# Four graph layers on one core: layer 1's activations from GpSimd with two column operands, orders drawn anew

## The reference

```python
h = jnp.maximum(_layernorm(x, axis=-1), 0.0)
x = x + _L0_gnn_ref(h, adj, ...)   # deg*(h Wi + b) + adj @ (h Wj)
h = jnp.maximum(_layernorm(x, axis=-1), 0.0)
x = x + _L1_gnn_ref(h, adj, ...)   # graph attention: softmax(leaky(src_i + dst_j)) @ (h W)
h = jnp.maximum(_layernorm(x, axis=-1), 0.0)
x = x + _L2_gnn_ref(h, adj, ...)   # graph attention on 128 features, beside h W itself
h = jnp.maximum(_layernorm(x, axis=-1), 0.0)
x = x + _L3_gnn_ref(h, adj, ...)   # attention with 8 heads, masked by adj
```

## Time and profile before

| what | before |
|---|---|
| median of three runs | 1237.13 us (1236.1 to 1239.11) |
| profiled execution: its own time | 1239.31 us |
| profiled execution: span from first to last instruction | 1237.2 us, granted TensorE clock 0.994 |
| busy: PE, PEld | 1193.5 us (96%), 1101.4 us (89%) |
| busy: POOL | 1137.0 us (92%) |
| busy: ACT, DVE | 1099.5 us (89%), 1092.9 us (88%) |
| DMA | 78.59 MB, 64 GB/s in the mean |

### The profile page before, as it was taken

One profiled execution on the slowest core, in us unless ns is written; L12 is line 12 of the kernel. 1 busy time (PEld: TensorE's weight loads), 2 busy tenths in 40 slices (PEclk: granted clock), 3 DMA queues, 4 the chain that ended last, 5 costly groups with the idle time before them and its releaser, 6 DMA issues. The chain is left out here.

```text
span 1237.2 us, 44146 instructions
## 1 busy us (share of the span) xinstructions
PE 1193.5 (96%) x12017; PEld 1101.4 (89%) x12017; DVE 1092.9 (88%) x5524; ACT 1099.5 (89%) x4040; POOL 1137.0 (92%) x1857
## 2 busy tenths in 40 slices
PE   6889999999999999999999999999999999999997
PEld 5678999998999898998999999899989999999986
DVE  6889999989999898998999999899989999998773
ACT  3559999999999899998999998999989999999986
POOL 5989999999999999999999999999999999998774
PEclk9999999999999999999999999999999999999999
DMA  7220342433333344343343344244344234421001
GB/s 189 64 63 13 69 74 60 68 75 53 70 74 57 67 75 56 65 77 55 66 76 55 70 74 58 67 73 60 67 71 68 64 67 71 64 46 23 19 20 35
DMA packets 97682, 78.59 MB, mean 64 GB/s; under 512 B 31648, under 2 KB 89248, under 8 KB 97440
## 3 DMA queue, kind: packets, MB, share of 16 engines
q1 hardware_dynamic: 94960, 74.07, 32.9%
q10 hardware_dynamic: 2480, 1.71, 0.5%
HBM read 58.79 MB, written 16.95 MB: 61 GB/s over the span
## 5 line engine op out<-in xcount | busy, mean ns | idle before, releaser
L1347 ACT ACTIVATE exps<-masked,nmax 128x128 f32<-128x128 f32 x1024 | 398.0, 397 | 9.9 <-issue 6.7
L497 POOL TENSOR_TENSOR probs<-exps,rsum 128x512 f32<-128x512 f32 x256 | 266.6, 1043 | 14.9 <-DVE rsum L909 14.9
L901 DVE CUSTOM_DVE_ANT_0 masked<-bank,mask 128x128 f32<-128x128 f32 x1024 | 225.3, 285 | 6.7 <-PE bank L1736 6.2
L768 DVE BATCH_NORM_STATS2 stats<-x 128x6 f32<-128x256 f32 x512 | 187.9, 409 | 15.4 <-DMA x<-in_x 14.7
L1347 ACT ACTIVATION_READ_ACCUMULATOR exps<-masked,nmax 128x1 f32 x1024 | 200.2, 195 | 0.0
L1584 PE MATMUL bank<-w_hi,ht_hi 128*128 128x512 f32 (+1 forms) x508 | 184.5, 363 | 0.0
L430 POOL TENSOR_TENSOR rstd<-veps,power 128x2 f32<-128x2 f32 x256 | 182.3, 713 | 0.3
L1585 PE MATMUL bank<-w_lo,ht_hi 128*128 128x512 f32 (+1 forms) x508 | 172.0, 339 | 0.0
L1586 PE MATMUL bank<-w_hi,ht_lo 128*128 128x512 f32 (+1 forms) x508 | 171.7, 338 | 0.0
L461 POOL TENSOR_SCALAR y<-x,nm 128x256 f32<-128x256 f32 x128 | 146.6, 1154 | 6.0
L453 POOL TENSOR_SCALAR y<-x,nm,rstd 128x256 f32<-128x256 f32 x256 | 140.9, 557 | 11.3 <-issue 10.8
(11 more groups left out here) (140 smaller groups left out, 4108.4 us busy)
## 6 DMA issues: line engine op xcount, KB each, us to landing
x<-in_x SPq DMA_DIRECT2D x64, 256.0 KB, 5.6
xt_sb<-in_xt SPq DMA_DIRECT2D x64, 256.0 KB, 5.6
out<-x SPq DMA_DIRECT2D x64, 256.0 KB, 3.8
db<-rows SPq DMA_DIRECT2D x110, 128.0 KB, 4.1
mean_b<-rows SPq DMA_DIRECT2D x62, 128.0 KB, 3.5
rows<-mv SPq DMA_DIRECT2D x62, 1.0 KB, 5.6
rows<-logits SPq DMA_DIRECT2D x55, 1.0 KB, 5.1
rows<-dst SPq DMA_DIRECT2D x55, 1.0 KB, 3.8
```

The lines of the kernel that those rows point to most:

```text
L497: pool.tensor_tensor(probs3[:, p % BUFFERS["probs3"], j], exps3[:, p % BUFFERS["exps3"], j], rsum3[:, s, j].unsqueeze(2).to_broadcast([P, ...
L768: last = dve.bn_stats(stats[i][:, b, g], src[:, bx, g])
L901: last = dve.tensor_tensor_reduce(masked3[:, b, j, i], bank_of(f"sc{j}")[:, i * P:(i + 1) * P], mask[:], scale=-1.0, scalar=-MASKED, op0=A ...
L1347: last = act.activation(exps3[:, b, j, i], masked3[:, p % BUFFERS["masked3"], j, i], ACT.Exp, bias=nmax3[:, s, j, i:i + 1], scale=-1.0, ac ...
```

## The change

`centre1` computes the same `y1` in another form: the maximum of `x1` and the mean, minus the mean. Both operands are now the column of the mean in `mv1`, so `nm1` and its instruction are gone, and the buffers of `mv1` are freed by `y1` instead of `nm1`.

```diff
-        nm = [None] + [sb(f"nm{i}", [P, SMALL, G]) for i in range(1, 4)]
+        nm = [None, None] + [sb(f"nm{i}", [P, SMALL, G]) for i in (2, 3)]
...
             def centre1(p):
                 b, s, bx = p % BUFFERS["y1"], p % SMALL, p % BUFFERS["x1"]
-                passed(pool, "nm1", p)
+                passed(pool, "mv1", p)
                 read_before(pool, "y1", p, "dots1", "g1_mm")
                 for g in range(G):
-                    last = pool.tensor_scalar(y[1][:, b, g], x1[:, bx, g], nm[1][:, s, g:g + 1], 0.0, ALU.add, ALU.max)
+                    last = pool.tensor_scalar(y[1][:, b, g], x1[:, bx, g], mv[1][:, s, 0, g:g + 1], mv[1][:, s, 0, g:g + 1], ALU.max, ALU.subtract)
                 last.then_inc(S["y1"], 1)
...
-       "kt_mm": 5, "products": -1, "h0t": -12, "z2": 13, "mj_hi0": 8, "exp3_2": 15, "exp2": 13, "w3_high": 9, "z1": 10, "kt": 14,
+       "x4_mm": 7, "d2": 3, "m0": -2, "qt_mm": 4, "ot_hi": 16, "exp3_1": 14, "v": 14, "p3t_2": 15, "h3t_hi": 13, "p3t_1": 15, "at1": 10,
```

In `drain` on GpSimd, `biased_x3(NP - 2)` stood between scalings of the last pair and now stands ahead of all four:

```diff
+                biased_x3(NP - 2)
+                normalise_p3(2, NP - 1)
                 normalise_p3(1, NP - 1)
                 normalise_p3(3, NP - 1)
-                biased_x3(NP - 2)
-                normalise_p3(2, NP - 1)
                 normalise_p3(0, NP - 1)
                 biased_x3(NP - 1)
```

More of the change, by code:

```diff
@@ L296, in fill @@
                 load(3)
-                load(4)
                 write_means(2)
@@ L379, in _ @@
             fill()
-            for t in range(15, NP + 10):
+            for t in range(16, NP + 12):
                 step(t)
@@ L518, in fill @@
+                centre1(0)
+                low_w3(0)
                 shifted_variance(1, 0)
-                negative_mean(1, "y1", 0)
-                centre1(0)
-                inverse_deviation(0, 3)
+                subtract_means(2)
+                low_w3(3)
+                scaled_degree(2)
                 inverse_deviation(1, 0)
-                subtract_means(2)
-                scaled_degree(2)
+                scale_logits1(0)
+                scaled_degree(3)
+                biased_x0(3)
@@ L588, in fill @@
                 shifted_variance(2, 2)
-                centre1(5)
-                negative_mean(2, "y2", 2)
+                shifted_variance(1, 5)
+                inverse_deviation(2, 2)
                 clear_empty_rows(3)
-                inverse_deviation(2, 2)
                 normalise(2, x2, 2)
-                shifted_variance(1, 5)
-                x3_tail(1)
-                biased_x3(0)
                 inverse_deviation(1, 5)
                 inverse_deviation(0, 7)
+                subtract_means(7)
@@ L608, in fill @@
-                negative_mean(2, "y2", 3)
-                shifted_variance(2, 3)
-                inverse_deviation(2, 3)
-                negative_mean(1, "y1", 6)
-                shifted_variance(0, 8)
-                normalise(2, x2, 3)
-                shifted_variance(1, 6)
-                centre1(6)
+                biased_x3(0)
+                inverse_deviation(0, 8)
+                shifted_variance(2, 3)
+                negative_mean(2, "y2", 3)
+                inverse_deviation(2, 3)
@@ L616, in fill @@
+                normalise(2, x2, 3)
+                centre1(6)
+                x3_tail(2)
+                normalise_p3(2, 0)
+                shifted_variance(1, 6)
+                subtract_means(8)
+                inverse_deviation(1, 6)
+                normalise_p3(1, 0)
+                shifted_variance(3, 2)
+                scale_logits1(6)
                 shifted_variance(0, 9)
-                inverse_deviation(1, 6)
-                subtract_means(8)
-                scale_logits1(6)
@@ L631, in fill @@
+                inverse_deviation(2, 4)
+                negative_mean(2, "y2", 4)
                 normalise_p3(0, 0)
-                shifted_variance(2, 4)
+                normalise(2, x2, 4)
+                scaled_degree(8)
+                centre1(7)
+                normalise_p3(1, 1)
             def drain():
-                normalise_p3(1, NP - 3)
                 biased_x3(NP - 3)
@@ L688, in step @@
                     shifted_variance(3, t - LAG["veps3"])
+                if due(t, "veps0") and t > LAG["veps0"]:
+                    shifted_variance(0, t - LAG["veps0"])
                 if due(t, "nm3"):
@@ L713, in _ @@
             fill()
-            for t in range(6, NP + 2):
+            for t in range(4, NP + 0):
                 step(t)
@@ L1210, in _ @@
             fill()
-            for t in range(11, NP + 7):
+            for t in range(12, NP + 8):
                 step(t)
@@ new lines, in fill @@
+                high_mj(0, 8)
+                exps3_of(2, 1)
+                exps(2, "rsum2", 3)
+                add_key_bias(2)
+                relu_transposed2(4)
+                copy_exp_transposed(2, 3)
+                copy_p3_transposed(3, 0)
+                copy_p3_transposed(0, 0)
+                sum_logits(1, logits1[:, (6) % SMALL, 0], 6)
+                high_g1(5)
+                copy_projection2(4)
+                exps(1, "rsum1_any", 6)
+                relu_difference(9)
@@ L1934, in step @@
                     project_transposed("qt", wq_r, t - LAG["qt_mm"])
-                if due(t, "kt_mm"):
-                    project_transposed("kt", wk_r, t - LAG["kt_mm"])
             idle_products(16)
             fill()
-            for t in range(8, NP + 4):
+            for t in range(7, NP + 3):
                 step(t)
```

785 lines of the change are left out of this document (389 added, 396 removed), and 24 rows, old and new, of the table LAG.

## The result

The changed kernel takes 1256.82 us in the median of four runs (1253.92 to 1258.39), the kernel before in the same set 1236.62 (1233.99 to 1239.11): a ratio of 1.0151, interval 1.0129 to 1.0173. The forecast was 1225 us; the sign is wrong. The profiled execution has a span of 1256.3 us at a granted clock of 0.992, 19.1 us above the one before.

The account below looks back on a forecast made before the run. Late rows of layer 2 and, less, POOL's pace hold rounds above PE's; POOL leads at the start. Middle 5.1 + start 6 + end 1 = 12.1 us off 1239.3 gives 1227.2, on the median's scale 1225 us, range 1212 to 1236.

Parts of the forecast that it names:

- the sign: Whole kernel: the change was forecast to make it faster, 1225 us; faster by over 0.3% had chance 0.77, slower 0.10.
- What bounds the kernel: Rounds of pairs 2 to 55: 17.9 us above PE's pace, 15.2 from late rows, 2.7 from POOL's slower pace.
- late rows: Layer 2 rows spread by DMA, awaited by ACT at line 1316 for `db`: 15 waits, 27.1 us together.
- The new form: `centre1` on POOL: 557 ns instead of 1154, negative mean gone, 1.53 us saved a pair; bounds 0.34 and 1.53.
- The rival of the slow maximum: `centre1` on POOL still costs 1154 ns, saving 0.34 us a pair: 1232 us on the median's scale; chance 0.15.
- The middle: Rounds between start and end: 2.7 us from POOL's pace plus 2.4 from late rows, 5.1 us gained; bounds 0 to 17.9.
- The 0.79 us per late row: Column `dst` on POOL: with 1.35 us of slack it starts sooner after ACT's copy, gaining up to 0.79 us.
- SyncE: SP's queue: load of `x` now directly ahead of the spread of layer 2's row; cost taken as zero.
- The row of layer 2 that comes late: SP's queue: the load delays the spread, 15 late rows cost 20 us more, 1250 us on the median's scale; chance 0.10.
- The start: Before layer 3's first scaling at 88.33 us: POOL gets there sooner, 6 us gained; bounds 0 and 9.2.
- The end: Last chain: `biased_x3` of pair 62 moved ahead of two scalings of pair 63, 1 us gained, 1.2 at most.
- PE's own round: PE's round without idle time: stays at 18.09 us; the prediction is wrong if it does not.

Follow-up runs that it names:

- the exchange back: Changed kernel with ScalarE's copy `hh` ahead of `h0r` again: 1230.94 us, ratio 0.9965; the same with before's form and its negative mean: 1241.71 us, ratio 1.0047.
- the cheap form: Changed kernel with add and multiply in place of maximum and subtract in `centre1`, for time only: 1213.37 us, ratio 0.982.
- the run with the load first: Changed kernel with SyncE's load of `x` ahead of the row write of layer 1 again: 1252.23 us, ratio 1.0146.

## Why the prediction was wrong

**What bounds the kernel.** That GpSimd's own round was longer than PE's was read rightly. The split of the 17.9 us above PE's pace, 15.2 for late rows and 2.7 for GpSimd, holds as a tally of PE's rounds: 14 of the 53 are longer than 18.40 us and have 15.4 us beyond PE's pace, and 27 are at most 18.15. It fails as a forecast of what a faster GpSimd brings. With GpSimd's round below PE's, and ACT's waits for late rows nearly as many (20.6 us in 16), 10.9 of the 17.9 were gone and 7.0 left. After a late row GpSimd does have a lead, as the prediction says: behind the one of the earlier trace rows PE's next rounds take 18.12, 18.11 and 18.09 us. But in the same stretch `centre1` comes back after 18.28, 18.30 and 18.26 us, so PE only uses up the lead and then waits for GpSimd again. GpSimd's own pace says it at once: its 968.3 us are 9.5 above PE's, and 8.4 are left for everything else.

**The new form.** This step failed first. It chose 557 ns because operand kinds and tile were the same "and only the arithmetic differs". The arithmetic was the price: 1227 ns. It also excluded anything above 1154, without a row. The saving was 0.34 - 0.15 = 0.19 us a pair, not 1.53, and GpSimd's round stayed the bound. The rival of the slow maximum was near in price and gave 1232, though a maximum is not what makes a pair slow. With this price and before's order the time is 1226; the rival failed here by what follows.

**The middle.** This step carries the sign. It saw that ScalarE's rectification moved ahead of the copy, and priced it at 0.63 us of margin for each late row. It did not ask what the rectification itself waits for, which is GpSimd's own subtraction. The loop subtraction, `h0r`, `hh`, `dst` put 0.33 us of waiting into each round of GpSimd, 24 to 26 us in the whole by the exchange back. The prediction expected POOL to wait for `hh` in nearly every round, and it does, but it counted on 1.35 us of slack there. With the cheap form the same waits are free. The 0.79 us per late row that this slack was to bring had no slack to come from.

**Also moved, and costed at nothing:** `y3` right behind its inverse deviation, 0.16 us of a round on GpSimd, some 5 to 6 us with the remainder of the order.

**SyncE.** Zero was right for the time: 1.0146 and 1.0151 with the load in either place. The row of layer 2 that comes late, which was the one rival on the slow side and gave 1250, came near the measured time with a mechanism that the run with the load first does not bear out.

**The start.** 6 us were forecast, and pair 2 came 0.4 us later. With the cheap form it comes at 141.88, 10.8 us sooner, beyond the bound of 9.2; the term hung on the price of the form. But the way was not the one forecast: even there layer 3's first scaling, which was to come 5 to 9 us sooner, starts at 86.50 us, 1.8 sooner. Where the rest of the 10.8 comes from isn't followed here. In the changed kernel that scaling starts at 94.25 us, where it was 88.33:

```profile
94.25 1.04 POOL L499 TENSOR_TENSOR probs<-exps,rsum 128x512 f32<-128x512 f32 x1
```

**The end.** 1 us was forecast; from pair 55 on it is 107.97 us after and 107.85 before. The kernel before and the one with only `h0r` moved ahead have the same end and differ here by 1.2 us (107.85 and 106.65), so a term of this size can't be seen.

**PE's own round,** which was to stay at 18.09 us, is 17.99 in the new order (with the cheap form, and in single rounds with `hh` first); why, no run shows. A kernel bound by GpSimd doesn't see this gain.

## What to carry to other kernels

When two instructions of an engine change places, follow both ends: what does the one that is now ahead wait for, and who waits for the one that is now behind. If the two ends lie on the same engine, and that engine sets the round, the work between them enters its round, less what stands there to cover it. Take an instruction's price from a row with the same operations, not the same shape, and where there is none, let the bounds go beyond the nearest row; before a stall is blamed for time above the pace, subtract what the second engine's pace explains on its own. And before work moves to another engine, look at what runs beside it there: an instruction's shortest time may not be the one that you get.

## What the hardware showed

On GpSimd, an instruction over 128 x 256 in fp32 with two operations cost 473 ns (add, multiply, one column and a constant; 556 with two columns) or 1145 to 1239 (add and maximum, maximum and subtract, maximum and add, subtract and multiply, subtract and maximum), with one operation, a maximum, 922. A second column in place of a constant added 83 ns. Multiplying by 1.0 behind a subtraction costs 2.4 times what it costs behind an addition (1155 against 473), so an addition of a negative mean made elsewhere can be the cheaper way where a multiplication follows. On GpSimd `y` started 0.17 us after the end of the inverse deviation that it reads when that stood right ahead of it; with another instruction between them there was no gap. On VectorE, one instruction of 128 x 256 (subtract, maximum) took 0.34 to 1.46 us: in 60 of 64 cases it ended 0.35 us after its start or 0.15 us after the end of the GpSimd instruction that was under way when it started, whichever was later.
